# A bias sum moved from TensorE to Pool, gate weight sums moved behind the softmax shift, and split keys loaded in another order

## The reference

```python
x = x + xattn(layernorm(x), ctx, ctx, Wq, bq, Wk, bk, Wv, bv)   # softmax(q k^T / sqrt(512)) v
x = x + attn(layernorm(x), ...)      # sigmoid((q k^T - thresh) * sharp) * gate_q * gate_k, 16 heads of 32
x = x + ffn(layernorm(x), gate_w, w_gate, w_up, w_down)          # top 1 of 8 experts
```

## Time and profile before

| | us |
|---|---|
| median of 3 runs | 362.3 (362.24 to 365.04) |
| the profiled execution | 361.52 |
| its span, from the first to the last instruction | 359.8 |
| TensorE busy | 322.9 (90%) |
| VectorE busy | 158.6 (44%) |
| ScalarE busy | 92.4 (26%) |
| Pool busy | 77.8 (22%) |
| mean granted TensorE clock | 0.991 of full |

### The profile page before, as it was taken

The page is one execution under the profiler, slowest core; times in us unless marked ns, Lnnn a source line. Parts: engine busy times, 40 slices in busy tenths (PEclk is TensorE's granted clock), DMA queues, the critical chain, the costliest instruction groups (busy, mean ns, idle before and its releaser), DMA issues. The chain is left out here.

```text
span 359.8 us, 5533 instructions
## 1 busy us (share of the span) xinstructions
PE 322.9 (90%) x1998; PEld 179.9 (50%) x1998; DVE 158.6 (44%) x349; ACT 92.4 (26%) x213; POOL 77.8 (22%) x84
## 2 busy tenths in 40 slices
PE   0997987989998799999999999999889997789993
PEld 1786654623544554354564354653434777633330
DVE  3205248505344657265467425541453555125331
ACT  1233210235112443411436321251401600010110
POOL 4000022640013400220700112302321600501212
PEclk9999999989999999999999999999999999999998
DMA  7999999999999904999930999630595061550010
GB/s 259 385 322 178 193 379 321 188 207 387 368 180 172 152 0 175 366 320 189 187 49 4 338 373 220 220 132 0 211 422 244 2 232 59 159 195 30 28 54 9
DMA packets 54694, 71.14 MB, mean 198 GB/s; under 512 B 2791, under 2 KB 33543, under 8 KB 53649
## 3 DMA queue, kind: packets, MB, share of 16 engines
q1 hardware_dynamic: 53120, 66.09, 68.1%
q0 software_dynamic: 1552, 4.78, 3.7%
HBM read 67.71 MB, written 3.67 MB: 198 GB/s over the span
## 5 line engine op out<-in xcount | busy, mean ns | idle before, releaser
L1159 PE MATMUL ST<-CTX_sb,PR_sb 128*64 128x512 f32 (+1 forms) x208 | 49.4, 617 | 2.4 <-ACT PR_sb L328 2.4
L765 DVE STREAM_TRANSPOSE CT_sb<-FF_sb 128x1024 f32<-128x1024 f32 x30 | 35.3, 1219 | 23.4 <-DMA FF_sb<-ctx 18.1
L1134 PE MATMUL SC<-CT_sb,qcurP_sb 128*64 128x256 f32 x240 | 31.5, 389 | 3.7 <-DVE CT_sb L765 3.7
L1159 PEld LDWEIGHTS ST<-CTX_sb,PR_sb 128*64 128x64 f32 (+1 forms) x208 | 14.5, 140 | 26.9 <-issue 24.8
L1054 PE MATMUL TR<-ident_sb,CTX_sb 128*128 128x128 f32 (+1 forms) x176 | 22.5, 269 | 4.3 <-ACT CT_sb L321 2.4
L1054 PEld LDWEIGHTS TR<-ident_sb,CTX_sb 128*128 128x128 f32 (+1 forms) x176 | 18.2, 142 | 12.0 <-issue 6.0
L1134 PEld LDWEIGHTS SC<-CT_sb,qcurP_sb 128*64 128x64 f32 x240 | 15.2, 136 | 16.5 <-issue 6.1
L1059 PE MATMUL A<-AW_sb,normT_sb 128*128 128x512 f32 x48 | 22.0, 600 | 0.0
L321 DVE COPY CT_sb<-TR 128x512 f32<-128x512 f32 (+1 forms) x22 | 14.2, 644 | 15.7 <-PE TR L1054 14.7
L494 POOL TENSOR_TENSOR rn_sb<-ss_sb,nhalf_sb 128x16 f32<-128x16 f32 x4 | 11.6, 2907 | 40.3 <-DVE ss_sb L842 40.3
L321 ACT COPY CT_sb<-TR 128x512 f32<-128x512 f32 (+1 forms) x22 | 12.0, 546 | 28.4 <-PE TR L1054 28.4
(11 more groups left out here) (242 smaller groups left out, 494.5 us busy)
## 6 DMA issues: line engine op xcount, KB each, us to landing
CTX_sb<-ctx SPq DMA_DIRECT2D x24, 1024.0 KB, 9.8
FF_sb<-ctx SPq DMA_DIRECT2D x32, 256.0 KB, 7.7
FF_sb<-ctx SPq DMA_DIRECT2D x56, 128.0 KB, 6.6
CTX_sb<-wgu SPq DMA_DIRECT2D x4, 1024.0 KB, 9.8
CTX_sb<-wdn SPq DMA_DIRECT2D x5, 512.0 KB, 12.6
FF_sb<-wgu SPq DMA_DIRECT2D x2, 1024.0 KB, 6.5
rows<-XR_sb SPq DMA_DIRECT2D x3, 512.0 KB, 10.1
CTX_sb<-ctx SPq DMA_DIRECT2D x8, 130.0 KB
```

The costliest lines, as they stand in the source:

```text
L765: v.transpose(ctxT[:, pos % 2, k, :, :].rearrange("p c (b r) -> p b c r", r=Q), split[:, k, at:at + BLOCKS, :].rearrange("p b (c r) -> p b ...
L1134: last = t_.matmul(out[q, :], (qcurP if split_group else qcur)[:, c, q], ctxT[:, pos % 2, k, c, 0:n], start=(c == 0), stop=(c == DC - 1))
L1159: last = t_.matmul(ST[q, :], probs[0:w, t, q], ctxb[0:w, k, t, :], start=(t == 0), stop=(t == KT - 1))
```

## The change

Three parts.

1. c is computed on Pool and TensorE: Pool multiplies the projected queries of each of the 4 feature chunks (128x512, all pairs) by bk's column and adds them up in `qbk` (the buffer of `vs`; `qbm`, the second, is that of `qh`); TensorE then needs one matmul with a column of ones for each pair instead of four with bk. The Pool operations stand right behind `pair_queries(0)`. `pair_bias(0)` moves ahead of the gate products.
2. VectorE's gate weight sums move from the end of the scores to behind the shift and the first copy of numerators.
3. `next_split(0)` loads part 0 as soon as two split groups of pair 0 are transposed, and part 1 after the third.

```diff
+        qbk, qbm = vs_own, qh
+        ones32 = sb("ones32", [P, 1])
@@ next_split (SyncE)
+                if is_first(p):
+                    sp.wait_ge(s["keysT_made"], split_turned(0, 2))
+                    load_split(1, 0)
+                    sp.wait_ge(s["keysT_made"], split_turned(0, 3))
+                    load_split(1, 1)
+                    return
@@ gpsimd
+            g.memset(ones32[:], 1.0).then_inc(s["const_made"], 1)
...
             pair_queries(0)
 
+            pool.wait_ge(s["vec_in"], 16)
+            pool.wait_ge(s["qp_moved"], 2 * DC)
+            for c in range(DC):
+                dst = qbk[:, :] if c == 0 else qbm[:, :]
+                if c >= 2:
+                    pool.wait_ge(s["bk_sum"], c - 1)
+                g.tensor_tensor(dst, qpT[:, c, :], vec[:, 1, c:c + 1].to_broadcast([P, D]), ALU.mult).then_inc(s["bk_mul"], 1)
+                if c:
+                    pool.wait_ge(s["bk_mul"], c + 1)
+                    g.tensor_tensor(qbk[:, :], qbk[:, :], qbm[:, :], ALU.add).then_inc(s["bk_sum"], 1)
+
+            pair_bias(0)
             pool.wait_ge(s["rowv_in"], 16)
...
-            pair_bias(0)
@@ vector
                 move_keys(dve, v.tensor_copy, 0, 1, FIRST.tile(u))
-                for n in range(2 * (u - (2 * GROUPS - DC)), 2 * (u - (2 * GROUPS - DC)) + 2):
-                    if n >= 0:
-
+            shift(0)
+            for c in range(1, NCH, 2):
+                move_numerators(dve, v.tensor_copy, 0, c)
+                if c == 1:
+                    for n in range(2 * DC):
                         dve.wait_ge(s["gmul"], n + 1)
                         at = HEADS * (n // DC)
                         v.tensor_reduce(wgate[...], (sq, kh)[n % 2]..., AX.X, ALU.add).then_inc(s["gred"], 1)
-            shift(0)
-            for c in range(1, NCH, 2):
-                move_numerators(dve, v.tensor_copy, 0, c)
                 turn_split(1, NEXT.groups[c // 2])
@@ tensor
-            pe.wait_ge(s["vec_in"], 16)
+            pe.wait_ge(s["bk_sum"], DC - 1)
             for p in range(PAIRS):
-                for c in range(DC):
-                    last = t_.matmul(AB[1][:, p:p + 1], qpT[:, c, p * P:(p + 1) * P], vec[:, 1, c:c + 1], start=(c == 0), stop=(c == DC - 1))
+                last = t_.matmul(AB[1][:, p:p + 1], qbk[:, p * P:(p + 1) * P], ones32[:], start=True, stop=True)
```

More of the change, by code:

```diff
@@ L253, in program @@
             half_made part_made const_made bias_made ln0_eps ln0_pow xn_made xnT_turned xnT_made
-            qp_made qp_moved qk_made qk_moved c_made c_moved gmul gred masks_zeroed
+            qp_made qp_moved bk_mul bk_sum qk_made qk_moved c_made c_moved gmul gred masks_zeroed
             qcur_made qcurP_made ccur_made keysT_made turned0 turned1 moved0 moved1 scored shift_made exp_made pv_chunk rsum_made on_made on_turned pvt_made
@@ L924, in choose @@
                 v.tensor_scalar(pick[:, i, :], iotaS, slot[:, i:i + 1], None, ALU.is_equal).then_inc(s["pick_made"], 1)
-            dve.wait_ge(s["const_made"], 8)
+            dve.wait_ge(s["const_made"], 9)
             dve.wait_ge(s["vec_in"], 16)
@@ L1048, in _ @@
             t_ = nc.tensor
-            pe.wait_ge(s["const_made"], 8)
+            pe.wait_ge(s["const_made"], 9)
             def turn_rows(bank, rows, n, w=P):
```

## The result

The changed kernel took 364.22 us (median of 17 executions, 362.92 to 365.75), the kernel before 362.24 in the same rounds. The ratio is 1.0073 with a 95% interval of 1.0052 to 1.0095: slower by 0.7%, within the 1% that the prediction called no change. Forecast were 364.1 us and a first pair 4.8 us late. The profiled execution of the changed kernel took 363.42 us (span 361.7) against 361.52 (span 359.8).

What follows compares the result with a forecast made beforehand. TensorE, busy nine tenths of the span, was taken as the bound, with DMA pacing the second pair twice. Profiled 361.52 us plus 1.8 gives 363.3, plus 0.8 for the median 364.1; 8-in-10 range 360.6 to 365.9.

Steps and rivals of the forecast that it cites:

- The copies' wait: First pair, after 33.6 us: VectorE's last four small query copies wait for Pool's operations and end 3.1 us late.
- 4.3 us bound: Bound of the copies' wait: four Pool operations and a short tail, if no copy slips in between.
- The lower clock: TensorE's clock falls behind its 4.2 us wait for the first turned keys (35.41 before), costing 1.7 us.
- D: Delay of the first pair: 3.1 us of copies' wait plus 1.7 of lower clock, 4.8 us.
- TensorE's lead: At the turn of the first pair's attention rows (88.49 before): 3.3 us earlier, with D left out.
- The clock that stays up: TensorE's first weighing (73.47 before): without the 1.55 us wait ahead of it, full clock wins 1.7 us.
- the ones product: TensorE's 32 one-column matmuls behind the scores (from about 61.7 us) become 8: 2.8 us less.
- The split loads: First split loads issued at 62.0 instead of 59.84, 2.2 us later; DMA stream 1.8 us late.
- price of the hole: Gap in the DMA stream at 60 to 63 us, share 0.65: its missing share is worth 1.3 us.
- The sum: DMA's delay of 1.8 us at the chunk (95.01) and split part (109.45) stays to the end: +1.8 us.
- Rival B: Pool's products don't hold VectorE's copies off, D = 0; TensorE then waits for its chunk: 361.0 us, chance 0.20.
- Rival A: Same copies' wait at TensorE's first turned keys but no lower clock, D = 3.1: 362.4 us, chance 0.22.

Runs made afterwards that it cites:

- four colliding operations: Changed kernel (364.22 us; again 364.74), kernel before with bias sum on Pool alone (368.83), changed kernel with chunk 0 loaded last (360.99): four VectorE copies meet Pool operations.
- two or none: Changed kernel, Pool waiting for VectorE's 16 small query copies behind its first two products (two: 363.49 us) or before all seven operations (none: 363.71, again 363.28).
- second profile: The changed kernel measured once more, nothing changed in it: 364.74 us, ratio to the kernel before 1.0057.
- the one with chunk 0 last: Changed kernel, chunk 0 of each later pair's context loaded behind chunks 1 to 3 and the last split part: 360.99 us, ratio to kernel before 0.9985.
- The parts alone: Kernel before with one part each: bias sum on Pool 368.83 us, order of split loads 361.74, gate sums behind the shift with bias copy ahead 361.02.
- the kernel without the collision: Changed kernel, but Pool's seven operations wait until VectorE's 16 small query copies are done: 363.71 us, again 363.28; ratios to kernel before 1.0022 and 1.0040.

## Why the prediction was right, step by step

- **The copies' wait** (3.1 us forecast): right in kind, 3.46 measured (7.77 - 4.31). The step "copy 3 slips into the gap in which the first sum waits for its semaphore" failed: it waited 1.31 us for the sum. All four waited for one operation each, as in the 4.3 us bound; the total came near the forecast because a product with bk's column takes 1.03 us, not the gate product's 1.27.
- **The lower clock** (1.7): right behind that wait it fell in every profile with four colliding operations and in none with two or none. From the first copy to the first split transpose, the changed kernel took 26.51 us instead of 21.55: D = 4.96 (4.8 forecast), of which 5.0 - 3.5 = 1.5 is the clock. In its second profile D was 5.6. What no step had is a second fall at 57 to 63, in three of the four profiles with four colliding operations (0.58 and 0.60 in 60 to 63, 0.63 in the one with chunk 0 last).
- **TensorE's lead** (3.3): too small. From the last split group's scores to the turn of the attention rows it took 24.44 us instead of 28.70: 4.3. The term was the chain of VectorE behind the sums. The sums took 8.9 us as forecast (9.0) but began 0.6 sooner, because the weighing did and the copy ahead of them overlaps its start; the copies and transposes behind them overlap at their ends (0.3). The reciprocal and ScalarE's step took the 1.1 forecast.
- **The clock that stays up** (1.7 of that lead): right in size, but for half a reason. The first weighing came 4.4 us sooner (4.0 forecast) and at full clock. The prediction put the fall in the kernel before down to the wait of 1.55 us alone. The parts alone show that without that wait the clock falls all the same, behind the 32 products with one column; it took the ones product to keep it at 1.00. The prediction had counted that part at 2.8 us and no clock.
- **The split loads** (issued 2.2 us later, stream +1.8): counted from the first copy, issued 2.4 and 3.0 us later than before (61.05 and 62.98), landed 0.8 and 1.8 late, part 2 transposed 0.9 and 1.9 late. Right in kind; two executions of one kernel differ by as much as the step. A deeper hole goes with a later issue (DMA share in 60 to 63: 1.23 with the issue at 56.83, 0.29 at 61.05, 0.12 at 62.98). But nothing shows the price of the hole, 1.3 us for closing it: in the one profile with the order of the loads alone it closed, and part 2 came 0.1 us earlier.
- **The sum** (+1.8): 1.9 at the end of the second pair in the second profile, by the way forecast. In the first it was 2.5, of which 0.9 came from the landing and 1.6 from the fall of the clock at 121, which no step had. The step "behind it TensorE sets the pace by itself, so +1.8 stays to the end" failed: the gather was issued later behind its indices and the last stage grew in the second profile (both below). That the total fits is chance in part; the ratio over all executions carries it.
- **Rival B** (361.0 without a collision) failed in its size. Its mechanism is there (1.86 and 1.98 us of waiting for context), yet the kernel without the collision took 363.3 to 363.7. Rival A's question is answered for this place: 2.6 us of waiting did not lower the clock, 4.5 did. It is no rule by length: elsewhere the clock was lower behind a wait of 1.55 us and behind some near 2 us.

What stays open: why the kernel without the collision is not faster than the kernel before. Part 2 was transposed 1.5 us earlier in one profile and 0.6 later in the other, so the second pair brought little. The rest of what the profiles show lies at the end of the kernel. In the four profiles without the bias sum on Pool the first gather is issued 1.10 us behind its indices and TensorE waits 1.5 to 1.6 us for the rows at full clock; the last stage then takes 51.7 to 51.8 us. In the nine with it the gather is issued 1.3 to 1.8 us behind them, with nothing in the profile that Pool waits for, TensorE waits 1.9 to 2.5 us, and in all but the first profile of the change the clock falls and the stage takes 53.2 to 54.7. In the second profile of the change:

```profile
318.00:321.00 3.00, 3.00 (x12) 0.92 (x10) 0.00 (x0) 0.00 (x0) 0.00 (x0) 0.69 0.97 384
```

Both together make 1.6 to 3.7 us in these eight profiles, at a place where no step of the prediction looked. The loss goes with the bias sum on Pool; what in that part brings it is not shown, and executions without a profile may have it in either kind of kernel.

## What to carry to other kernels

An idle engine's queue isn't free: look at what VectorE does while Pool would work, and count each SBUF-to-SBUF copy that meets a Pool operation as long as that operation. Before an engine's chain is shortened, look for the transfer it will then wait for; here the order of the loads brought 1.0% with the kernel before, and the shortened chain nothing that the times show. Compare profiles from a common event and not from their zero: starts differed by 1.5 us here, as much as the effects. A gain and a loss that both end in one wait for a transfer can't be told apart by the time.

## What the runs showed of the hardware

- A VectorE instruction with two small SBUF operands (128x1) took 1.13 us beside a Pool product, and 0.16 in the kernel before, where Pool was idle then. By the Trainium skill (SBUF — State Buffer, Who interferes with whom) a VectorE instruction with two SBUF inputs contends with a GpSimd one that reads SBUF: the trace agrees. VectorE's sums from one SBUF input were not held off (0.69 us beside a product, as in the earlier trace rows).
- Among back-to-back Pool operations without a wait, a waiting copy gets in between two of them: it waited 0.97 us, one product, not two.
- TensorE's clock fell behind 32 one-column products, with no wait between, in three of the four profiles that have them (0.58, 0.53 and 0.54 in 66 to 69); in the fourth, of the kernel before, it was 1.00 there. The nine with 8 of them kept 1.00 behind these.
- The lower clock cost 1.7 us each in three places: 7.10 us instead of 5.41 for the other pairs' queries, 5.35 instead of 3.65 for a weighing, and 5.35 instead of 3.65 for the first expert matmuls behind the gather (the change again, against the kernel before).
